# Solving the recurrence for x over its gate, and gating on VectorE as X is written

## The reference, cut to what matters

```python
def step(St, inp):
    q_t, k_t, v_t, a_t, b_t = inp
    err = einsum('bhvk,bhk->bhv', St, k_t) - v_t
    St = a_t[..., None] * St - (b_t[..., None] * err)[..., None] * k_t[:, :, None, :]
    o_t = einsum('bhvk,bhk->bhv', St, q_t)
    return (St, o_t)
```

## Time and profile before

| | |
|---|---|
| median of 3 runs | 2797.2 us (2792.12 to 2802.65) |
| the profiled execution: its time, its span | 2792.46 us, 2790.7 us |
| busy over the span: PE, VectorE, ACT, POOL | 92%, 73%, 43%, 52% |
| L1197 and L1202 on VectorE | 1792 instructions each, 328.5 and 330.8 us |
| L787 on POOL | 448 instructions, 331.6 us |
| mean granted clock of TensorE | 0.968 |

### The profile page before, as it was taken

How to read it: one execution, slowest core, us unless ns; L and a number is a source line. 1 busy time by engine, 2 the same in 40 slices (tenths; PEclk the granted TensorE clock), 3 DMA queues, 4 the chain that set the end, 5 groups by cost and what they waited for, 6 DMA issues and landing times. The chain is left out here.

```text
span 2790.7 us, 50619 instructions
## 1 busy us (share of the span) xinstructions
PE 2578.7 (92%) x17812; PEld 2216.3 (79%) x17922; DVE 2042.4 (73%) x5887; ACT 1204.5 (43%) x2393; POOL 1445.2 (52%) x1216
## 2 busy tenths in 40 slices
PE   8999999999999489999999999999749997899999
PEld 6888888888888378888888888888637776788887
DVE  4776778678769279999999999989768886433333
ACT  4445445544454233333333333323568874433333
POOL 2644553455355489999889898979422220000000
PEclk9999999999999799999999999989859999999999
DMA  5466555655664855555556566555654543100000
GB/s 132 129 177 185 150 146 163 187 143 146 171 179 124 266 201 215 200 198 198 215 227 231 214 230 227 214 197 198 240 202 158 213 188 122 67 12 11 11 11 15
DMA packets 417321, 454.39 MB, mean 163 GB/s; under 512 B 122497, under 2 KB 367233, under 8 KB 393857
## 3 DMA queue, kind: packets, MB, share of 16 engines
q1 hardware_dynamic: 417152, 452.22, 48.6%
HBM read 321.49 MB, written 131.14 MB: 162 GB/s over the span
## 5 line engine op out<-in xcount | busy, mean ns | idle before, releaser
L355 PE MATMUL pa_ps<-pa_x_hi,pa_w_hi 128*128 128x512 f32 x1296 | 507.0, 391 | 9.4 <-ACT pa_y L298 5.2
L355 PE MATMUL pa_ps<-pa_x_lo,pa_w_hi 128*128 128x512 f32 x1296 | 505.1, 390 | 0.0
L355 PE MATMUL pa_ps<-pa_x_hi,pa_w_lo 128*128 128x512 f32 x1296 | 504.9, 390 | 0.0
L438 DVE SCALAR_TENSOR_TENSOR pa_cv<-pa_y,pa_taps,pa_cv 128x2048 f32<-128x2048 f32 x144 | 357.1, 2480 | 17.8
L1197 DVE TENSOR_TENSOR pb_tmp<-pb_gb,pb_ps 128x112 f32<-128x112 f32 (+6 forms) x1792 | 328.5, 221 | 25.5 <-POOL pb_gb L787 11.6
L787 POOL TENSOR_TENSOR pb_gb<-pb_gb,pb_ng 128x448 f32<-128x448 f32 (+6 forms) x448 | 331.6, 786 | 2.9 <-DMA pb_gb<-scratch_pairs 2.9
L1202 DVE TENSOR_TENSOR pb_ps<-pb_ps,pb_tmp 128x112 f32<-128x112 f32 (+6 forms) x1792 | 330.8, 226 | 0.0
L355 PEld LDWEIGHTS pa_ps<-pa_x_hi,pa_w_hi 128*128 128x128 f32 x1296 | 243.6, 188 | 67.1 <-ACT pa_y L298 9.4
L771 POOL TENSOR_TENSOR all_res<-all_res,pb_crow 128x1024 f32<-128x1024 f32 x120 | 281.9, 2367 | 6.1 <-DMA pb_crow<-scratch_crow 6.1
L355 PEld LDWEIGHTS pa_ps<-pa_x_hi,pa_w_lo 128*128 128x128 f32 x1296 | 243.7, 188 | 50.7
L355 PEld LDWEIGHTS pa_ps<-pa_x_lo,pa_w_hi 128*128 128x128 f32 x1296 | 243.6, 188 | 50.0
(11 more groups left out here) (191 smaller groups left out, 5426.9 us busy)
## 6 DMA issues: line engine op xcount, KB each, us to landing
pb_crow<-scratch_crow SPq DMA_DIRECT2D x30, 2048.0 KB, 10.0
pb_gb<-scratch_pairs SPq DMA_DIRECT2D x64, 896.0 KB, 6.6
pa_o_ng<-scratch_beta SPq DMA_DIRECT2D x16, 1024.0 KB, 7.9
scratch_ng<-pa_o_ng SPq DMA_DIRECT2D x16, 1024.0 KB, 4.5
scratch_A<-pa_o_A SPq DMA_DIRECT2D x16, 1024.0 KB, 4.5
scratch_vt<-pa_o_vt SPq DMA_DIRECT2D x16, 1024.0 KB, 4.5
scratch_q<-pa_o_q SPq DMA_DIRECT2D x16, 1024.0 KB, 6.9
scratch_g<-pa_o_g SPq DMA_DIRECT2D x16, 1024.0 KB, 7.8
```

What stands on the lines that cost most here:

```text
L355: last = nc.tensor.matmul(out, w[:, mat, k, :], xx[:, k, b * S:(b + 1) * S], start=(k == 0 and n == 0), stop=(k == KT - 1 and n == 2))
L438: nc.vector.scalar_tensor_tensor(out=out, in0=yy[:, :, k:k + S], scalar=tap(k), in1=out, op0=ALU.mult, op1=ALU.add).then_inc(s_tap, 1)
```

## The change

Instead of x the solve now finds y, which is x over its gate: y_t = w_t plus the sum over s of y_s times (gate of s times the inner product of s and t). So `with_gates` multiplies each pair by the gate of the earlier step, the one that it comes from, which is one value for all pairs of an instruction and is passed as a broadcast operand. `solve` works in place on the right side (`y_of`), without the multiplication ahead of it. At its end VectorE multiplies y by the gates and writes the block of `X` itself, in SBUF, and counts `s_xc`. ACT's copy is gone; `copy_x` is now `transposed_x` and keeps only the copies of the transposed tiles. SP's load of `ng` and ACT's `ngx` wait for the new multiplication (`gated`) where they waited for the old one (`scaled`).

```diff
-        w_of = [t[:, 0:HALF * BL].rearrange("p (h t) -> p h t", t=BL) for t in wx]
-        x_of = [t[:, HALF * BL:2 * HALF * BL].rearrange("p (h t) -> p h t", t=BL) for t in wx]
+        y_of = [t[:, 0:HALF * BL].rearrange("p (h t) -> p h t", t=BL) for t in wx]
...
-        scaled = lambda c, n, hf: 27 * turn(c, n, hf) + 1
+        gated = lambda c, n: NBL * c + n + 1
...
-                sp.wait_ge(s_sv, scaled(c, 3, 0))
-                sp.wait_ge(s_sv, scaled(c, 1, 1))
+                sp.wait_ge(s_xc[0], gated(c, 3))
+                sp.wait_ge(s_xc[1], gated(c, 1))
                 load(ng[:, :, :], "ng", c + 1, s_ngl)
...
-                    last = tt(pairs, pairs, ng[:, :, BL * n + t + 1:BL * (n + 1)], ALU.mult)
+                    last = tt(pairs, pairs, ng[:, :, BL * n + t:BL * n + t + 1].broadcast_to([P, HB, w]), ALU.mult)
...
-            def copy_x(at, past, c, n, hf, between=None):
+            def transposed_x(at, past, c, n, hf, between=None):
 
-                act.wait_ge(s_x[hf], solved(c, n))
-                nc.scalar.activation(X[:, HALF * hf:HALF * (hf + 1), BL * n:BL * (n + 1)], x_of[hf], ACT.Copy).then_inc(s_xc[hf], 1)
                 if between:
                     between()
...
                 if kind != FIRST:
-                    act.wait_ge(s_sv, scaled(c - 1, 3, 1))
+                    act.wait_ge(s_xc[1], gated(c - 1, 3))
                 nc.scalar.activation(ngx[:, :, :], ng[:, HALF:HB, CH // 2:CH], ACT.Copy).then_inc(s_ngx, 1)
...
                 if n == 0:
                     dve.wait_ge(s_w, 2 * c + hf + 1)
-                    dve.wait_ge(s_ngl, 16 * (c + 1))
                 else:
                     dve.wait_ge(s_wn[hf], 6 * c + 2 * n)
-                gates = ng[:, HALF * hf:HALF * (hf + 1), BL * n:BL * (n + 1)]
-                if hf and n >= NBL // 2:
-                    dve.wait_ge(s_ngx, c + 1)
-                    gates = ngx[:, :, BL * n - CH // 2:BL * (n + 1) - CH // 2]
-                ws, xs = w_of[hf], x_of[hf]
-                tt(xs, ws, gates, ALU.mult).then_inc(s_sv, 1)
+                ys = y_of[hf]
                 dve.wait_ge(s_m, NBL * c + n + 1)
-                dve.wait_ge(s_sv, 27 * k + 1)
...
-                        tt(xs[:, qs, t + 1:BL], xs[:, qs, t + 1:BL], tmp[:, hs, 0:w], ALU.add).then_inc(done, 1)
+                        tt(ys[:, qs, t + 1:BL], ys[:, qs, t + 1:BL], tmp[:, hs, 0:w], ALU.add).then_inc(done, 1)
+                if n == 0:
+                    dve.wait_ge(s_ngl, 16 * (c + 1))
+                gates = ng[:, HALF * hf:HALF * (hf + 1), BL * n:BL * (n + 1)]
+                if hf and n >= NBL // 2:
+                    dve.wait_ge(s_ngx, c + 1)
+                    gates = ngx[:, :, BL * n - CH // 2:BL * (n + 1) - CH // 2]
+                dve.wait_ge(s_x[hf], solved(c, n))
+                tt(X[:, HALF * hf:HALF * (hf + 1), BL * n:BL * (n + 1)], ys, gates, ALU.mult).then_inc(s_xc[hf], 1)
```

More of the change, by code:

```diff
@@ L909, in last_key @@
                     copy_key(at - T_CH, T_FIRST[1][1], 0, 1, 1)
-                copy_x(at, past, c, 0, 0, last_key if kind != FIRST else None)
+                transposed_x(at, past, c, 0, 0, last_key if kind != FIRST else None)
                 key(T_LATER, 1, 0, 0)
@@ L915, in cycle @@
                 if kind != FIRST:
-                    copy_x(at, past, c - 1, 3, 1, lambda: next_gram(0))
+                    transposed_x(at, past, c - 1, 3, 1, lambda: next_gram(0))
                 else:
@@ L920, in cycle @@
                 absolutes(1)
-                copy_x(at, past, c, 1, 0, lambda: next_gram(2))
+                transposed_x(at, past, c, 1, 0, lambda: next_gram(2))
                 next_gram(3)
@@ L925, in cycle @@
                 if kind != FIRST:
-                    act.wait_ge(s_sv, scaled(c - 1, 3, 1))
+                    act.wait_ge(s_xc[1], gated(c - 1, 3))
                 nc.scalar.activation(ngx[:, :, :], ng[:, HALF:HB, CH // 2:CH], ACT.Copy).then_inc(s_ngx, 1)
-                copy_x(at, past, c, 2, 0)
+                transposed_x(at, past, c, 2, 0)
                 absolutes(3)
-                copy_x(at, past, c, 0, 1, lambda: key(T_LATER, 1, 1, 0))
+                transposed_x(at, past, c, 0, 1, lambda: key(T_LATER, 1, 1, 0))
                 key(T_LATER, 1, 1, 1)
@@ L934, in cycle @@
                 absolutes(4)
-                copy_x(at, past, c, 3, 0, (lambda: copy_kt(1)) if more else None)
+                transposed_x(at, past, c, 3, 0, (lambda: copy_kt(1)) if more else None)
                 if more:
@@ L939, in cycle @@
                 absolutes(5)
-                copy_x(at, past, c, 1, 1, (lambda: key(T_FIRST, 0, 0, 0)) if more else None)
+                transposed_x(at, past, c, 1, 1, (lambda: key(T_FIRST, 0, 0, 0)) if more else None)
                 absolutes(6)
@@ L944, in cycle @@
                     key(T_FIRST, 0, 1, 0)
-                copy_x(at, past, c, 2, 1)
+                transposed_x(at, past, c, 2, 1)
                 absolutes(7)
@@ L956, in _ @@
             over_cycles(act, cycle)
-            copy_x(T_START + T_CH * NCH, {}, NCH - 1, 3, 1)
+            transposed_x(T_START + T_CH * NCH, {}, NCH - 1, 3, 1)
             for k in range(SUMS[-1], 4 * PIECES):
@@ L1016, in x_transposes @@
                     busy(bank_t(at, t), fill)
-                pe.wait_ge(s_xc[hf], NBL * c + n + 1)
+                pe.wait_ge(s_xc[hf], gated(c, n))
                 if n:
@@ L1172, in first_v @@
                 dve.wait_ge(s_de, at + D_S[4 * hf + 3] + 1 + 4)
-                tt(w_of[hf], w_of[hf], vt[:, HALF * hf:HALF * (hf + 1), 0:BL], ALU.subtract).then_inc(s_w, 1)
+                tt(y_of[hf], y_of[hf], vt[:, HALF * hf:HALF * (hf + 1), 0:BL], ALU.subtract).then_inc(s_w, 1)
             def solve(c, n, hf, early=0):
@@ L1195, in solve @@
                         if t:
-                            dve.wait_ge(s_sv, 27 * k + 1 + 4 * (t - 1) + 2 + q + 1)
-                        tt(tmp[:, hs, 0:w], gb[n][:, hs, off[t]:off[t] + w], xs[:, qs, t:t + 1].broadcast_to([P, QUART, w]),
+                            dve.wait_ge(s_sv, 26 * k + 4 * (t - 1) + 2 + q + 1)
+                        tt(tmp[:, hs, 0:w], gb[n][:, hs, off[t]:off[t] + w], ys[:, qs, t:t + 1].broadcast_to([P, QUART, w]),
                            ALU.mult).then_inc(s_sv, 1)
                     for q, qs, hs in quarters:
-                        dve.wait_ge(s_sv, 27 * k + 1 + 4 * t + q + 1)
+                        dve.wait_ge(s_sv, 26 * k + 4 * t + q + 1)
                         done = s_sv if w > 1 else s_x[hf]
-                        tt(xs[:, qs, t + 1:BL], xs[:, qs, t + 1:BL], tmp[:, hs, 0:w], ALU.add).then_inc(done, 1)
+                        tt(ys[:, qs, t + 1:BL], ys[:, qs, t + 1:BL], tmp[:, hs, 0:w], ALU.add).then_inc(done, 1)
[7 more added lines that the diff above has]
+                tt(X[:, HALF * hf:HALF * (hf + 1), BL * n:BL * (n + 1)], ys, gates, ALU.mult).then_inc(s_xc[hf], 1)
             def cross(at, past, c, n, hf, p):
@@ L1215, in cross @@
                     dve.wait_ge(s_wv, 2 * c + hf + 1)
-                    tt(w_of[hf], w_of[hf], W[:, hs, BL * (n + 1):BL * (n + 2)], ALU.add).then_inc(s_wn[hf], 1)
+                    tt(y_of[hf], y_of[hf], W[:, hs, BL * (n + 1):BL * (n + 2)], ALU.add).then_inc(s_wn[hf], 1)
             def state(at, c, r):
```

4 lines of the change are left out of this document (2 added, 2 removed).

## The result

The changed kernel takes 2780.82 us, median of 15 runs (2770.16 to 2782.18); the kernel before, beside it, 2789.98 us (2781.3 to 2802.65). The ratio is 0.9955, with a 95% interval from 0.9945 to 0.9966: the change saves 0.34% to 0.55%, which is 9.5 to 15.3 us. It was forecast to save 5. Of all executions that this document counts with, one of e3 ran in a slower state and is left out.

The account below looks back on a forecast made before the run. VectorE and PE were taken to lead a 64.2 us chunk by turns. PE's wait for X (3.8 us) plus VectorE's solves (1.3 us) gave 5 us off the 2797.2 us median: forecast 2792, range 2776 to 2815.

Parts of the forecast that it names:

- both waits and all solves count: Rival: both PE waits for X and all eight solves' savings count, 1.1 us a chunk, 18 us, 2779; chance 0.18.
- The loop: VectorE leads from solve (c,0,1) through (c,1,1), PE behind that; the delay to X counts once, in (c,0,0).
- Head: VectorE at a solve's start: first product directly behind L1216 without the multiplication between, saving 0.46 to 0.53 us.
- Tail: VectorE at a solve's end: the new multiplication waits for the last sums, so the next operation starts 0.45 to 0.52 us later.
- The term of 1.3 us: VectorE's own time: 0.02 us net saved in each of four solves that count, over 16 chunks.
- The rule that the prediction took from the Trainium skill: VectorE: no step starts before the previous one's pipe is empty, so the solve's end costs what its start saves.
- X to PE: Solve (c,0,0): X comes 0.42 us earlier, PE's 0.24 us wait goes, the rest is lost; 3.8 us over 16 chunks.
- The load of the gates: SP's load of `ng`: issued 4.1 us later, landing 7.0 us after issue, POOL 2.0 us late, no cost to the time.
- 4.4 us: Lateness absorbed before VectorE reads block 2: 1.9 us from two POOL waits plus 2.5 us of slack.
- gates land too late: Rival at POOL's `with_gates(c+1, 0)`: load takes 10.7 us, VectorE waits 1.3 us in each of 15 chunks, 2812; chance 0.15.
- POOL's broadcast: POOL's gating with one gate per head as operand: -0.5 to +0.2 us for one gating, taken as 0 to the path.
- ACT: 128 copies of 0.38 us go, 49 us of an engine idle two thirds of the time; no gain.

Follow-up runs that it names:

- e3: The kernel before, with the copy of X moved from ACT to VectorE and the gating still ahead of the solve: 2838.8 us, ratio 1.0143.
- e1: The kernel before, with only POOL's gating operand made a broadcast (each pair gated by the earlier step): 2792.7 us, ratio 0.9997.
- e2: The changed kernel, with POOL's gating operand put back to a run instead of a broadcast: 2776.9 us, ratio 0.9948 to the kernel before.
- e4: The changed kernel without the multiplication of y by the gates, ACT copying y to X: 2773.7 us, ratio 0.9938 to the kernel before.
- e5: The changed kernel, waiting for the last sums first and for the gates' semaphores behind that: 2775.7 us, ratio 0.9932 to the kernel before.
- e8: The changed kernel, with the load of `ng` moved behind those of `gb` and `kq`: 2849.2 us, ratio 1.0191 to the kernel before.

## Why the prediction was right, and where it was not

**The time.** Forecast 2792 against a base of 2797.2, measured 2780.82 against 2789.98. The direction was right; the gain is 9.2 us by the medians and 9.3 by the regular chunk, and was put at 5.1. Of the 11 us by which the time itself was off, 7 are the base, a median of three runs. The measured time stands nearest to the rival "both waits and all solves count" (2779), but that is the base's doing: the rival wanted 1.1 us a chunk, and 0.62 came.

**The loop.** That VectorE leads from (c,0,1) to (c,1,1), that PE leads behind that, and that X counts in solve (c,0,0), is borne out: the chunk fell in A by about what VectorE saves there and in B by what X is earlier. POOL's operand has no part in it (e1 and e2), and e4 shows how near PE is in A.

**Head and tail.** Head: 0.46 to 0.53 saved, measured 0.53. Tail: 0.45 to 0.52 more. Measured: from the last pair's start to the next operation 0.68 us with one wait and 0.75 with a wait for the gates ahead of it, where it was 0.22, so 0.46 or 0.53. I took 0.02 net for every solve; it is 0.07 for the solves that wait once and 0 for those with two waits, 64 and 63 of the 128 tails (one took 0.76 to its multiplication). e5 makes them all alike. Part A holds two of each among its solves, 0.14 us; measured 0.19. The term of 1.3 us was 3 us.

The rule that the prediction took from the Trainium skill (VectorE: DVE Perf Modes, "The DRAIN you can't avoid") would have given a net of zero. Against it stands part A, 0.19 us shorter, and that L1208 starts at 1408.17, 0.08 us before L1200 of 0.42 us has ended, as L1216 did in the earlier trace rows. The prediction gave that section shorter than it is: it also says that a next operation which is not held starts earlier, and these rows are in line with that sentence.

**X to PE: the step that failed.** "PE's wait for X in solve (c,0,0) is 0.24 us. It goes whole, and the rest of the 0.42 is lost, since then PE arrives last." That X comes 0.42 us earlier was right: from the start of the `cross` products ahead to the start of the transposes it was 5.30 us (1229.62 to 1234.92) and is 4.90 (1429.37 to 1434.27). But next to none of it was lost: part B fell by 0.42. The price was 0.24 x 16 = 3.8 us where it should have been 0.42 x 15 = 6.3. The row of 0.24 begins where the last filler is modelled to end (0.38 us long, while its weights were ready much earlier and another matmul of the kind could follow at 0.22), and so hides the first part of the wait. Counted from there PE lost 0.40 us. The weight load's own wait, 0.73 us, was in the same trace, and I had not read it. It says that there is more than 0.24 to be had, but it overstates: of the 0.32 us that are left of it nothing more can be won while the fillers stand, since the transposes start at 5.08 us behind L1170 in e4 and e5 as well, where X is 0.11 and 0.07 earlier. That X is earlier by just what PE was kept waiting is a coincidence of two lengths, and the next step of this kind is worth little.

**The load of the gates.** Issued 4.1 us later: 4.2. Landing 7.0 us behind the issue: 4.8. Of its waits for this load POOL shows 0.9 us in the whole recurrence, where I had 2.0 in each chunk. That the load does not matter was right, and would have been right with a landing of 7.0 too: block 0's pairs are ready at 1423.7 (half of the 9.93 us behind 1418.74) and first read at 1429.66, so POOL could have started 5.9 us later before VectorE waited there. But I had followed only the queue behind the gating, not the gating's own first reader. It is where e8 waits, with POOL 6.7 to 8.0 us late, and hardly at block 2, whose 4.4 us no run contradicts. The rival "gates land too late" had POOL 5.7 us late, which is just inside that room, and its 20 us for it are tested by no run; e8's delay cost 68.

**POOL's broadcast.** Predicted -0.5 to +0.2 us for a gating, taken as 0 to the path: 5.02 against 5.19 us, and nothing to the path. The Trainium skill (GPSIMD Engine Reference, "Elementwise — side-by-side cycle accounting") has a floor by which a broadcast would buy nothing; here it buys 12 us of POOL's time (331.6 to 319.0), none of which the loop sees.

**ACT.** Nothing, as forecast: 35 us less in 1000 us, in an engine that idles.
